# Reordering the second attention step of a fused cross-attention and 4-bit MLP kernel: key and query logits ahead of the denominators

## The reference, cut to what matters

```python
x = x + tanh(g_xattn) * xattn(layernorm(x), ctx)      # x, ctx: 32 batches of 64 x 512
x = x + tanh(g_ffn) * ffn(layernorm(x))               # 4-bit weights, 512 -> 1376 -> 512, silu gate

def xattn(q, k=v=ctx):                                # linear attention, 8 heads of 64, n = 512
    qh, kh, vh = Wq q, Wk k, Wv v                     # per batch: (512 x 64) @ (64 x 512)
    qh = softmax(qh, over the 64 channels of a head) * 64 ** -0.5
    kh = softmax(kh, over the 512 columns)
    context = kh @ vh.T                               # 64 x 64 per head
    out = Wo (context.T @ qh) + bo
    return out / norm(out, over channels) * g * 8
```

## Time and profile before

| | |
|---|---|
| three runs | 671.38, 672.50, 672.38 us; median 672.38 |
| the profiled execution | 672.23 us, its span 670.2 us |
| busy in the span | PE 651.4, DVE 581.7, ACT 488.8, POOL 257.4 us |
| mean granted TensorE clock | 0.994 of full speed |

### The profile page before, as it was taken

The page is one execution under the profiler, slowest core; times in us unless marked ns, Lnnn a source line. Parts: engine busy times, 40 slices in busy tenths (PEclk is TensorE's granted clock), DMA queues, the critical chain, the costliest instruction groups (busy, mean ns, idle before and its releaser), DMA issues.

```text
span 670.2 us, 14346 instructions
## 1 busy us (share of the span) xinstructions
PE 651.4 (97%) x5097; PEld 342.9 (51%) x5097; DVE 581.7 (87%) x819; ACT 488.8 (73%) x860; POOL 257.4 (38%) x352
## 2 busy tenths in 40 slices
PE   7899999999999999999999999999999999999996
PEld 5554564555465465456456454444544544454443
DVE  7777898898898898889889749899999899988996
ACT  4786777677677678678677665788877887777775
POOL 6312323214223223232235373565444444444442
PEclk9999999999999999999999999999999999999998
DMA  4112312421430320221220000000001000000102
GB/s 118 36 32 77 99 50 57 101 64 41 100 90 13 101 80 6 85 81 32 57 81 24 6 8 3 1 1 1 1 16 48 1 0 33 33 0 5 43 17 63
DMA packets 30619, 28.58 MB, mean 43 GB/s; under 512 B 18623, under 2 KB 20810, under 8 KB 30578
## 3 DMA queue, kind: packets, MB, share of 16 engines
q1 hardware_dynamic: 28170, 27.37, 14.8%
q10 hardware_dynamic: 2408, 0.70, 0.4%
HBM read 22.06 MB, written 4.23 MB: 39 GB/s over the span
## 4 chain that ended last, share of the span: by engine, by line
PE 87%; ACT 5%; DVE 4%; issue 1%; POOL 1%; DMA 1%; SPq 1%; DVEq 0%; POOLq 0%
PE small L1061 8%; PE pair L1344 8%; PE pair L1133 8%; PE small L1027 7%; PE pair L1345 7%; PE pair L1013 6%; PE pair L1358 6%; PE pair L1367 6%; PE small L1045 4%; ACT eq L674 4%; PE small L1344 4%; PE pair L1158 4%; PE small L1345 4%; PE pair L992 3%; PE small L1099 3%; PE pair L1143 2%
## 5 line engine op out<-in xcount | busy, mean ns | idle before, releaser
L1747 DVE SCALAR_TENSOR_TENSOR acc<-pair,scale_T,acc 128x512 f32<-128x512 f32 (+1 forms) x176 | 126.7, 747 | 12.2 <-ACT acc L809 6.4
L835 ACT ACTIVATE pair<-pair,rescale 128x512 f32<-128x512 f32 x119 | 74.9, 656 | 39.4 <-PE pair L1367 39.4
L1358 PE MATMUL pair<-in_hi,d_int 128*128 128x512 f32 (+1 forms) x176 | 100.8, 575 | 0.4 <-ACT in_hi L824 0.4
L1367 PE MATMUL pair<-in_lo,d_int 128*128 128x512 f32 (+1 forms) x176 | 100.3, 573 | 0.0
L665 ACT ACTIVATE ek<-pair,kneg 128x512 f32<-128x512 f32 x128 | 86.4, 682 | 19.0 <-DVE kneg L1607 19.0
L1344 PE MATMUL pair<-ek,w_gu 128*128 128x512 f16 (+1 forms) x235 | 91.1, 388 | 1.0 <-DVE acc L1747 0.7
L1345 PE MATMUL pair<-ekT,w_gu 128*128 128x512 f16 (+1 forms) x235 | 89.1, 379 | 0.0
L573 POOL TENSOR_TENSOR inter<-act_gate,acc 128x512 f32<-128x512 f32 (+1 forms) x43 | 54.9, 1277 | 87.6 <-ACT act_gate L817 87.6
L1612 DVE TENSOR_TENSOR eq<-eq,pair 128x1024 f32<-128x1024 f32 x64 | 77.7, 1215 | 11.1 <-PE pair L1118 10.8
L1602 DVE TENSOR_REDUCE qmax<-pair 128x16 f32<-128x1024 f32 x64 | 78.2, 1221 | 8.6 <-PE pair L992 7.5
L1607 DVE TENSOR_REDUCE kneg<-pair 128x2 f32<-128x1024 f32 x64 | 77.9, 1217 | 0.9 <-PE pair L1013 0.7
(11 more groups left out here) (198 smaller groups left out, 1331.6 us busy)
## 6 DMA issues: line engine op xcount, KB each, us to landing
xall<-in_x SPq DMA_DIRECT2D x16, 256.0 KB, 2.7
ctx_raw<-in_ctx SPq DMA_DIRECT2D x16, 256.0 KB, 3.0
out_x<-xall SPq DMA_DIRECT2D x16, 256.0 KB, 2.0
zero<-zeros_plus SPq DMA_DIRECT2D x8, 344.0 KB, 5.2
packed<-in_L_ffn_gate_qweight SPq DMA_DIRECT2D x4, 688.0 KB
packed<-in_L_ffn_up_qweight SPq DMA_DIRECT2D x4, 688.0 KB
packed<-in_L_ffn_down_qweight SPq DMA_DIRECT2D x10, 256.0 KB
zero<-zeros_plus SPq DMA_DIRECT2D x5, 256.0 KB, 4.6
```

Source lines behind the costliest of these rows:

```text
L1358: pe.matmul(z_bank[nt], d_int[0:w, it, nt * P:(nt + 1) * P], in_hi[0:w, n % 2, :], start=it == 0, stop=False, skip_group_check=True)
L1367: pe.matmul(z_bank[nt], d_int[0:w, it, nt * P:(nt + 1) * P], in_lo[0:w, n % 2, :], start=False, stop=True, skip_group_check=True).then_inc ...
L1747: dve.scalar_tensor_tensor(out=acc[0:w, n % 2, m, :], in0=gu_bank[(8 * n + job) % 3][0:w, :], scalar=scale_T[0:w, it, 4 * m + g:4 * m + g ...
```

## The change

Only step 1 is reordered; no instruction is added or removed, and steps 0 and 2 to 16 keep their order.

- PE: `k_logits(0)`, `t_logits(2)` and `k_transposed(3, back=1)` now stand ahead of `denominators`. Further on, `k_logits(1)` stands ahead of `context(0)`, and `t_logits(3)` and `k_logits(3)` change places with `context(1)` and `context(2)`.
- ACT: `k_transposed(3, back=1)` and `k_exps(0)` now stand ahead of the copy of the denominators, the gates behind it.
- DVE: `k_maxima(0)` moves ahead of `layernorm_apply(2)`, and `k_maxima(2)` ahead of `reciprocals`; `q_maxima(3)` stays behind `reciprocals`.

```diff
@@ ScalarE, step()
-                denominators()
-                if not residual:
+                if residual:
+                    denominators()
+                    k_exps(0)
+                else:
                     k_transposed(3, back=1)
-                k_exps(0)
-                if not residual:
+                    k_exps(0)
+                    denominators()
                     gates()
@@ TensorE, step()
                 if not residual:
+                    k_logits(0)
+                    t_logits(2)
+                    k_transposed(3, back=1)
                     denominators()
-                    k_logits(0)
-                    k_transposed(3, back=1)
-                    t_logits(2)
+                    k_logits(1)
                     context(0)
-                    k_logits(1)
-                    context(1)
                     k_logits(2)
                     t_logits(3)
+                    context(1)
+                    k_logits(3)
                     context(2)
-                    k_logits(3)
                     context(3)
                     q_max_rows()
                     q_logits(0)
@@ VectorE, step()
                 if combine and not residual:
+                    k_maxima(0)
                     layernorm_apply(2)
-                    k_maxima(0)
                     q_maxima(2)
                     k_maxima(1)
+                    k_maxima(2)
                     reciprocals()
-                    k_maxima(2)
                     q_maxima(3)
                     k_maxima(3)
```

## The result

The changed kernel takes 673.56 us (median of 13 runs, 672.71 to 675.47), the kernel before 671.53 us beside it (13 runs, 671.00 to 673.85). The ratio is 1.0029, 95% interval 1.0019 to 1.0039: slower by 1.3 to 2.6 us. The fastest runs differ by 1.71 us.

What follows compares the result with a forecast made beforehand. PE's dense work in step 1 and the denominator chain, ending within a quarter of a microsecond of each other, were taken as the bound. 2.10 - 0.06 - 0.44 = 1.60 us on 672.23 gave 673.8; 8-in-10 range 672.5 to 675.0.

Steps and rivals of the forecast that it cites:

- When ACT reaches the denominators: Step 1: ACT copies the denominators 2.03 to 2.16 us later, set by ACT and no longer by PE.
- my lower end: Step 1 on PE: the lower estimate for `t_logits(2)`, 0.27 us, of a range up to 0.40 us.
- How long the chain is: Step 1, denominators' copy to gather: 0.06 us shorter to the reciprocal, 0.44 by a shorter cast; the gather's 4.06 stays.
- the 0.06 that I took off: Step 1, copy to reciprocal: taken as 0.06 us shorter, from a possible 0 to 0.12 us.
- The sum: Delay of the gather and of step 1's end: 2.10 - 0.06 - 0.44 = 1.60 us, ends 1.47 and 2.16.
- the start of the sum: The profiled execution of the kernel before, 672.23 us, to which the forecast added 1.60 us.
- What hides it: Step 1 on PE: no work reaches the late gather, so PE waits about 1.2 us at the spread.
- regained in the second half: Rival, second half of step 1: 0.4 us of PE's idle time squeezed out, shift 1.2 us, 673.4; chance 0.26.
- A faster kernel by that order: Rival, step 1: the transfers don't gate and PE loses its waits, at most 1.22 us, 671.0; chance 0.08.
- The clock: Rival, step 1: the wait before the spread lowers PE's clock once, 1.7 us more, 3.3 in all, 675.5; chance 0.06.
- The fall at 14 us: Early stretch where the granted clock fell, 1.7 us lost; taken to agree with the skill's DMA waits dropping PE's rate.
- The rule of the Trainium skill: Step 1's transfers, issued later: by the rule alone the whole delay of the issue is paid, 2.1 us, 674.3.

Runs made afterwards that it cites:

- e5: The changed kernel with ACT's copy of the denominators ahead of `k_exps(0)`, still behind the transposed copy; ratio to the kernel before 1.0029.
- e1: The kernel before with only ACT's new order (transposed copy and key exponentials ahead of the denominators' copy); ratio 1.0061.
- e3: The kernel before with only `k_logits(0)`, `t_logits(2)` and `k_transposed(3, back=1)` put ahead of `denominators()` on PE; ratio 1.0022.
- e6: The kernel before with POOL's two low parts of step 1 exchanged, the context's first; ratio 0.9992.
- e10: The kernel before with POOL's two low parts of step 1 exchanged and `t_logits(2)` alone ahead of `denominators()` on PE; ratio 0.9997.
- e9: The changed kernel with the denominators' copy ahead of `k_exps(0)` on ACT and POOL's two low parts of step 1 exchanged; ratio to the kernel before 1.0051.
- e2: The kernel before with only DVE's new order (`k_maxima(0)` ahead of the layernorm, `k_maxima(2)` ahead of the reciprocals); ratio 1.0037.
- e4: The kernel before with only PE's later part: `k_logits(1)` ahead of `context(0)`, `t_logits(3)` and `k_logits(3)` earlier, denominators still first; ratio 1.0015.
- e8: The kernel before with PE's `fold_context` ahead of the first spread and query logits ahead of the later ones; ratio 0.9997.

## Why the prediction was right

- *When ACT reaches the denominators*, 2.03 to 2.16 us later: 4.11 - 2.04 = 2.07. ACT sets it, as predicted, but only the last 0.36 us of it: with the copy ahead of the exponentials (e5) it still starts at 3.75, when PE has the denominators. Two small errors cancel: `k_logits(0)` began 0.14 us after the exponential, not 0.05, and `t_logits(2)` took 0.23 us, less than my lower end. e1 and e3 show the term by itself: 3.63 us later gives a spread 3.21 later, 1.71 gives 1.27. The difference is 0.42 and 0.44, the cast.
- *How long the chain is.* From the copy to the reciprocal 36.82 - 31.92 = 4.90 us, against 4.89: the 0.06 that I took off isn't there; the first issue is 0.84 us long again, so that is step 1's own. From the reciprocal to the gather 37.89 - 36.82 = 1.07 against 1.50, 0.43 less, for 0.44. The gather 4.06, unchanged.
- *The sum*: 2.07 + 0.01 - 0.43 = 1.65 at the spread, for 1.60; the same 1.65 at step 2. That the total came out so near, 673.56 for 673.8, is partly luck: the start of the sum, 672.23, lay 0.70 us above the median of 671.53 measured beside the changed kernel, and the medians differ by 2.03, 0.43 more than the sum.
- *What hides it*: `context(0)`, the transposed maxima and the wait at the spread came where they were put (4.86, 11.33 and 1.16 us; forecast 4.7, 11.2 and 1.2). What the prediction did not say is that in the kernel before, too, the chain first held PE through `q_maxima(3)`, ahead of the gather (e6).
- *The rivals.* Nothing was regained in the second half, where PE's idle time stayed. A faster kernel by that order was not in sight: e6 and e10, which do shorten the chain and the gaps, gain 0.36 and 0.40 us in the trace and nothing that the total can tell. The clock did not fall in step 1 of the changed kernel's profile. But in e9 it did, at a price of 1.44 us, where I had 1.7; so the rival may have deserved more than the 0.06 it got, though a wait of 2.76 us in e1 and the waits of e2 left the clock full. The fall at 14 us, which the prediction set beside waits on a DMA, followed a wait for VectorE, 1.66 us for its query maxima ahead of 13.38 us; the trace does not bear out that part. In e9 the last wait ahead of the fall was for a DMA, the gather.

The rule of the Trainium skill that spoke against the change ("DMA: Bandwidth & Descriptors", section "Rules for kernel authors": issue early, wait late) held in its direction. Its price by the whole delay of the issue, 2.1 us, is what the copy's start shows (2.07); the trace has 1.65 at the end, because the later cast missed POOL.

The medians differ by 2.03 us, 0.38 more than the trace shows; the fastest runs differ by 1.71. Four runs of the changed kernel took 674.05 to 675.47 us. Over the whole execution their mean granted clock was 0.990 to 0.994, that of the nine faster ones 0.990 to 0.996, which does not single them out; whether the clock fell in step 1 of these can't be said, as only the profiled execution has a trace.

## What to carry to other kernels

Where a dense engine and a chain of small transfers meet at one instruction, look at both lengths before reordering: here they were 0.26 us apart, and in e1, e3 and the changed kernel each 1 us of delay at the chain's start cost 1 us, but for the 0.42 to 0.44 us of the cast. Work put ahead of the start of such a chain has to be free on every engine that the chain passes, not only on the busiest one; here PE's three pieces ahead of the denominators set 1.71 us of the 2.07, and two exponentials on an engine that was busy for 73% the last 0.36. Parts of a reordering don't add up: alone they cost 3.24, 2.16, 1.31 and 0.29 us at step 2, together 1.65.

## What the runs showed of the hardware

A small VectorE instruction can be stretched to the end of a GpSimd instruction. The cast, 0.195 us else, took 0.63, 1.05, 0.57, 0.62, 0.68 and 0.23 us in the kernel before, e2, e4, e8, e9 and e5, and ended 0.05 or 0.06 us behind GpSimd's each time; the subtraction with two SBUF operands took 1.22 instead of 0.225 us in e9 and ended 0.08 us behind GpSimd's next. The reciprocal beside them kept its 0.55 us while GpSimd ran. The Trainium skill states this in "SBUF — State Buffer", section "SBUF: two separate sides": VectorE's instructions in a two-port mode contend with GpSimd for a shared port pair, as do those with two SBUF inputs when GpSimd's reads SBUF, and whoever starts first holds the pair for the whole instruction. The runs agree in that each time GpSimd had started first and VectorE's instruction ended behind it; that the cast runs in a two-port mode is shown by none of them.
